# Gate's and up's LoRA by pairs of samples, with B's rows split once and gathered from a table in DRAM

## The reference

```python
# x: 32 samples x 64 positions x 512 features, all float32
x = x + L0(x)      # per sample a 64x64 matrix chosen by itok_B_0_7, and a bias
x = x + L1(x)      # the part that the change touches, adapters chosen by itok_B_0_7:
    base = x @ W ; lora = (x @ A[idx]) @ B[idx]      # rank 16, 8 adapters
    gate, up = lora_linear(x, Wg, Ag, Bg), lora_linear(x, Wu, Au, Bu)   # 512 -> 2048
    y = lora_linear(silu(gate) * up, Wd, Ad, Bd)                        # 2048 -> 512
x = x + L2(x)      # 512x512 matrix and rank-16 adapters chosen by itok_B_0_6
x = x + L3(x)      # per sample a 64x64 matrix chosen by itok_B_1_198
```

## Time and profile before

| | |
|---|---|
| median of 3 runs | 746.84 us (744.89 to 747.26) |
| the profiled execution: time, span | 746.99 us, 745.1 us |
| mean granted clock of TensorE in it | 0.984 |
| units 0 to 7, units 8 to 15 | about 52 to 335 us, about 361 to 635 us |
| before the first unit, and from the last unit on | 52 us, 110 us |

### The profile page before, as it was taken

The page is one execution under the profiler, slowest core; times in us unless marked ns, Lnnn a source line. Parts: engine busy times, 40 slices in busy tenths (PEclk is TensorE's granted clock), DMA queues, the critical chain, the costliest instruction groups (busy, mean ns, idle before and its releaser), DMA issues.

```text
span 745.1 us, 11097 instructions
## 1 busy us (share of the span) xinstructions
PE 713.5 (96%) x3762; PEld 611.7 (82%) x3762; DVE 583.8 (78%) x1008; ACT 289.7 (39%) x526; POOL 289.2 (39%) x537
## 2 busy tenths in 40 slices
PE   8789999999999999989899999999999999879997
PEld 8677788888888888868678888888888888669996
DVE  8868877888887888699898979797878795655553
ACT  3443423343334343334353333342424242335554
POOL 5936423242324232450337162525344331324541
PEclk9899999999999999999999999999999999989999
DMA  8485612121222121413723132222212142203432
GB/s 228 104 139 164 161 57 86 57 85 58 86 84 85 58 86 56 86 29 113 254 75 114 53 106 71 81 80 67 88 62 84 31 130 83 91 11 104 128 113 93
DMA packets 82024, 69.72 MB, mean 94 GB/s; under 512 B 43184, under 2 KB 65712, under 8 KB 81968
## 3 DMA queue, kind: packets, MB, share of 16 engines
q1 hardware_dynamic: 73328, 46.44, 21.5%
q0 software_dynamic: 8320, 22.56, 10.1%
q10 hardware_dynamic: 320, 0.02, 0.0%
HBM read 60.09 MB, written 8.91 MB: 93 GB/s over the span
## 4 chain that ended last, share of the span: by engine, by line
PE 81%; DVE 10%; issue 6%; ACT 2%; DMA 1%; POOL 0%; POOLq 0%; DVEq 0%; ACTq 0%
PE bank L1552 35%; PE bank L1673 21%; PE bank L1560 7%; PE bank L1683 4%; PE bank L1810 3%; PE bank L1816 3%; PE bank L1848 2%; PE bank L1789 1%; DVE XC L1040 1%; PE bank L1505 1%; DVE hid L1164 1%; PE bank L1529 1%; DVE hs L1170 1%; PE bank L1493 1%; DMA BR<-in_L_cond_Bu_dram,boffs 1%
## 5 line engine op out<-in xcount | busy, mean ns | idle before, releaser
L1552 PE MATMUL bank<-XC,WC 128*128 128x512 f32 x1344 | 333.3, 394 | 12.2 <-DVE XC L1040 4.6
L1552 PEld LDWEIGHTS bank<-XC,WC 128*128 128x128 f32 x1344 | 244.4, 189 | 60.8 <-issue 7.0
L1673 PE MATMUL bank<-hs,wds 128*128 128x512 f32 x768 | 190.6, 398 | 6.8 <-DVE wds L1123 4.1
L1673 PEld LDWEIGHTS bank<-hs,wds 128*128 128x128 f32 x768 | 145.2, 192 | 36.9 <-DVE wds L1123 4.5
L464 POOL DMA_INDIRECT BR<-in_L_cond_Bu_dram,boffs x64 | 72.5, 1132 | 253.0 <-DVE BL L1117 238.4
L464 POOL DMA_INDIRECT BR<-in_L_cond_Bg_dram,boffs x64 | 75.8, 1184 | 89.4 <-DVE BL L1117 73.6
L726 ACT ACTIVATE hs<-hid 128x512 fp32r<-128x512 f32 x64 | 40.3, 630 | 164.3 <-DVE hid L1164 109.1
L1181 DVE TENSOR_TENSOR XA<-bank,XA 128x512 f32<-128x512 f32 x128 | 86.4, 686 | 18.6 <-PE bank L1673 16.2
L720 ACT ACTIVATE hid<-hid 128x512 f32<-128x512 f32 x48 | 30.4, 633 | 152.6 <-DVE hid L1147 83.1
L1560 PEld LDWEIGHTS bank<-UT,BL 128*128 128x128 f32 x512 | 76.4, 189 | 9.6 <-issue 0.9
L1560 PE MATMUL bank<-UT,BL 128*128 128x256 f32 x512 | 81.7, 282 | 0.6 <-DVE BL L1117 0.4
(11 more groups left out here) (184 smaller groups left out, 874.7 us busy)
## 6 DMA issues: line engine op xcount, KB each, us to landing
RW<-in_L_cond_Wg_dram SPq DMA_DIRECT2D x16, 512.0 KB, 3.5
RW<-in_L_cond_Wu_dram SPq DMA_DIRECT2D x16, 512.0 KB, 3.5
RD<-in_L_cond_Wd_dram SPq DMA_DIRECT2D x16, 512.0 KB, 3.4
out_dram<-XB SPq DMA_DIRECT2D x16, 256.0 KB, 2.1
XB<-in_x_dram SPq DMA_DIRECT2D x8, 256.0 KB, 6.9
x1park<-XB SPq DMA_DIRECT2D x8, 256.0 KB, 5.0
x2park<-XA SPq DMA_DIRECT2D x8, 256.0 KB, 2.4
XA<-x1park SPq DMA_DIRECT2D x4, 512.0 KB, 6.9
```

What stands on the lines that cost most here:

```text
L1552: last = nc.tensor.matmul(psum[:, :], WC[:, t, left, a, k, :], XC[:, right, b, k, :], start=(first and k == 0 and n == 0), stop=(k == 1 an ...
L1673: last = nc.tensor.matmul(psD[j % 2][:, :], by_feature(wds[:, f, a, :])[:, j % KT, :], hs[:, f, b, j // KT * 512:(j // KT + 1) * 512], sta ...
```

## The change

B's rows are no longer split per window. The rows of Bg and Bu (128 rows of all 8 adapters) are split once per unit index 0 to 7, in one piece of 128x512 (`b_high(unit)`, `b_low(unit)`), and stored high and low to tables in DRAM (`load_b`, `store_b` on SP). `gather_b(b, half)` now fetches for every pair of samples 96 rows, which are high, low and high again of two samples by 16 ranks, straight into `BL`. `BL` has three places; a place holds the 4 pairs of half a window. `UT` holds 96 rows to match (high, high, low of u), so one matmul has all three terms: a call of `lora` is 4 matmuls of 128 columns with weights of 96x128. `select` makes 4 matmuls of 256 columns for what were 2 of 512. The second half of the tokens gathers from the tables that the first half stored.

Some small work moves too: the pair's row numbers are made early on DVE (`pair_rows`), layer 2's B is turned in unit 12 and loaded in unit 8, and `ident2` is made in unit 3.

```diff
-                def gather_b(b):
-                    unit, rows = b // 2, (bg_rows, bu_rows)[b % 2]
-                    if b:
-                        pool.wait_ge(s_bl, 2 * b)
+                def gather_b(b, half):
+                    unit = b // 2
                     h, i = unit // UNITS, unit % UNITS
-                    for q in range(HQ):
-                        at = HQ * h + q
+                    if half == 0 and h == 0 and b % 2 == 0:
+                        pool.wait_ge(s_bst, 32 * (unit + 1))
+                    if b == 0:
+                        if half == 0:
+                            pool.wait_ge(s_poffs, 1)
+                        else:
+                            pool.wait_ge(s_u, 1)
+                    elif half == 0:
+                        if b >= 2:
+                            pool.wait_ge(s_prod, 8 * (b - 2) + 8)
+                        if b == 2 * UNITS:
+                            pool.wait_ge(s_u, 3)
+                    else:
+                        pool.wait_ge(s_prod, 8 * (b - 1) + 7)
+                    place = b_place(b, half)                      # (2 * b + half) % 3
+                    for c in range(HP // 2):
+                        at = HP * h + HP // 2 * half + c
                         nc.gpsimd.indirect_dma_start(
-                            BR[:, q, :], None, rows,
-                            bass.IndirectOffsetOnAxis(boffs[:, at:at + 1].bitcast(u32), 0),
-                            element_offset=i * QT).then_inc(s_br[q // 2], 16)
+                            BL[0:PROWS, place, c, :].bitcast(f32), None, btab[b % 2][i],
+                            bass.IndirectOffsetOnAxis(poffs[0:PROWS, at:at + 1].bitcast(u32), 0)).then_inc(s_bin[place], 16)
...
-                def lora(psum, f, j, tok, first):
-                    for q in range(2):
-                        for a in range(2):
-                            last = nc.tensor.matmul(psum[:, q * QT:(q + 1) * QT], BL[:, a, 2 * tok + q, f * P:(f + 1) * P],
-                                                    UT[:, j, (2 * tok + q) * QT:(2 * tok + q + 1) * QT],
-                                                    start=(first and q == 0 and a == 0), stop=(q == 1 and a == 1),
-                                                    skip_group_check=True)
+                def lora(psum, f, j, tok, b, first):
+                    for c in range(HP // 2):
+                        p = HP // 2 * tok + c
+                        last = nc.tensor.matmul(psum[:, c * P:(c + 1) * P], BL[0:PROWS, b_place(b, tok), c, f * P:(f + 1) * P],
+                                                UT[0:PROWS, j, p * P:(p + 1) * P],
+                                                start=(first and c == 0), stop=(c == HP // 2 - 1), skip_group_check=True)
                     return last
...
-                    b_high(2 * unit + 1, 0)          # ACT, gate_window; b_low(2 * unit + 1, 0) on DVE alike
+                    if unit + 1 < UNITS:
+                        b_high(unit + 1)
```

More of the change, by code:

```diff
@@ L350, in x1_back, with load_b, store_b @@
                         sp.dma_start(XA[:, k, :], x1park[:, k, :]).then_inc(s_x1back, 16)
+                def load_b(unit):
+                    if unit == 1:
+                        sp.wait_ge(s_l0, PAIRS)
+                    elif unit:
+                        sp.wait_ge(s_bl, unit)
+                    for w in range(2):
+                        sp.dma_start(b_raw[min(unit, 1)][:, w, :], b_rows[w][:, unit * QT:(unit + 1) * QT]).then_inc(s_bld, 16)
+                def store_b(unit):
+                    sp.wait_ge(s_bl, unit + 1)
+                    for w in range(2):
+                        sp.dma_start(btab[w][unit].rearrange("(a p) f -> p a f", a=2),
+                                     b_split[min(unit, 1)][:, :, w, :].bitcast(f32)).then_inc(s_bst, 16)
                 load_idx(0, idx_a)
@@ L386, in _ @@
                         load_d(unit + 1)
+                    if unit + 1 < UNITS:
+                        store_b(unit + 1)
+                    if unit + 2 < UNITS:
+                        load_b(unit + 2)
                     if unit + 2 < ALL:
@@ L762, in up_window @@
                     hs_high(unit, 1, 0, 3)
-                    if unit + 1 < ALL and not turn:
-                        b_high(2 * unit + 2, 0)
                     hs_high(unit, 1, 1, 2)
@@ L780, in _ @@
                 xc_high(0, B21)
+                b_high(0)
                 sums_high(G, 0)
@@ L981, in move_matrices @@
                     dve.wait_ge(s_ident, 1)
-                    for half in range(2):
-                        rows = slice(half * POS, (half + 1) * POS)
-                        nc.vector.tensor_copy(ident2[rows, :], ident[rows, rows])
-                    link(nc.vector.memset(moves[:, :, :].bitcast(f32), 0.0))
-                    for j in range(2):
-                        last = nc.vector.tensor_copy(moves[:, 2 * j + 1, :], ident[:, j * HALF:(j + 1) * HALF])
+                    link(nc.vector.memset(moves[:, :, :, :].bitcast(f32), 0.0))
+                    for at in (0, 2):
+                        last = nc.vector.tensor_copy(moves[:, :, at, :], ident[:, :].rearrange("p (c m) -> p c m", c=4))
                     last.then_inc(s_moves, 1)
@@ L1008, in scalings @@
                     dve.wait_ge(s_l0, PAIRS)
+                    for half in range(2):
+                        rows = slice(half * POS, (half + 1) * POS)
+                        nc.vector.tensor_copy(ident2[rows, :], ident[rows, rows])
                     nc.vector.tensor_copy(idxb_f, idx[:, 1, :])
@@ L1220, in gate_window @@
                         hs_low(unit - 1, 0, 1, 4)
-                    b_low(2 * unit, 1)
                     raw_low(U, unit)
@@ L1237, in gate_window @@
                     evicts(unit, slots[1], 0)
-                    b_low(2 * unit + 1, 0)
+                    if unit + 1 < UNITS:
+                        b_low(unit + 1)
                     evicts(unit, slots[1], 1)
@@ L1247, in up_window @@
                         g_combine(unit + 1)
-                    b_low(2 * unit + 1, 1)
                     sum_u2(n)
@@ L1279, in up_window @@
                         xc_low(1, T3)
-                    if unit + 1 < ALL and not turn:
-                        b_low(2 * unit + 2, 0)
                     hs_low(unit, 1, 1, 3)
@@ L1318, in _ @@
                 xr_sum(4)
+                pair_rows()
                 xr_sum(5)
@@ L1324, in _ @@
                 xc_low(0, B21)
+                b_low(0)
                 t2_sum(0)
```

167 lines of the change are left out of this document (93 added, 74 removed).

## The result

The changed kernel takes 740.31 us (median of 4, 739.64 to 742.22) where the kernel before takes 746.27 (4 runs, 744.89 to 747.26): a ratio of 0.9926, 95% interval 0.9900 to 0.9951. The prediction was 740.8 us in a range of 736 to 747. Later the unchanged kernel was run again among the experiments: 739.87 us against 745.83, ratio 0.9921 (0.9906 to 0.9936).

A forecast was written before the change was run, and what follows sets the result against it. PE, busy 96%, was taken to bound the kernel, with DVE late at a few places. Terms -4.1 + 0.2 + 0.1 - 4.5 + 1.8 + 0.4 = -6.1 gave 740.8 us, range 736 to 747.

The forecast's parts named there:

- The columns: PE's `lora` calls: halved columns take each from 0.472 to 0.44 us, -4.1 us over 128 calls.
- the small corrections: On PE: +0.2 us for call gains lost ahead of waits for `sum_u3`, +0.1 for more matmuls in `select`.
- The step's argument: In `lora` calls, successive weight loads stand 100 to 110 ns apart, so matmuls of 60 ns between them don't help.
- DVE's relief: Fewer `b_low` instructions shorten PE's waits for DVE in units 0, 1, 4 and 8: -4.5 us.
- The start: `pair_rows` and `b_low(0)` on busy DVE ahead of the first S2·T2 make PE start later: +1.8 us.
- The gathers: POOL's doubled indirect DMAs fit by 1.3 to 1.9 us in windows without `downs`; one or two late: +0.4 us.
- the first: Rival for `lora` calls: columns are what is paid, -29.7 us instead of -4.1, 715 us; chance 0.05.
- The second: Rival on POOL: gathers are late and the kernel is slower, +12 us, 753 us; chance 0.11.
- the third: Rival: nothing is left; matmuls stay at 118 ns, DVE's relief is -2.2, the start +2.5, 747.4 us; chance 0.14.

The follow-up runs named there:

- e8: The changed kernel, unchanged, run again on another chip: 739.87 us, ratio 0.9921 to the kernel before.
- e3: The kernel before with 128 columns instead of 256 in each LoRA matmul: 742.96 us against 745.6, ratio 0.9956.
- e10: The kernel before with DVE's split of B cut from the second window on and LoRA matmuls at 128 columns instead of 256: 738.50 us, ratio 0.9901.
- e7: The changed kernel without its gathers of B from the fifth window on: 738.69 us, ratio 0.9916.
- e12: The changed kernel with 64 of 128 columns in each LoRA matmul, run again on a fourth chip: 740.72 us, ratio 0.9919.
- e2: The changed kernel with two matmuls of 256 columns a LoRA call instead of four of 128: 760.65 us, with long stalls.
- e9: The kernel before with DVE's split of B cut to 4 of 256 columns from the second window on: 741.07 us, ratio 0.9932.
- e5: The changed kernel with `pair_rows`, the first `b_low` and the first store of B's rows moved later: 739.79 us, ratio 0.9922.
- e1: The changed kernel with 64 of 128 columns in each LoRA matmul: 780.95 us, ratio 1.0455, with long stalls.
- e4: The changed kernel with an idle 512-element DVE instruction wherever the kernel before split B: 783.62 us with long stalls; 748.55 us on a third chip.
- e6: The changed kernel with two more gathers of 32 rows in each of POOL's calls: 763.87 us, ratio 1.0248.
- the first batch: The runs e1, e2, e3 and e4: 780.95, 760.65, 742.96 and 783.62 us; all but e3 had long stalls.

## Why the prediction was right

The medians fell by 5.96 us both times, where -6.1 was forecast. The trace of e8 against that of before, by the same matmuls, shows the terms. Its span is 8.1 us shorter. Of this 1.5 is a stretch of half clock in layer 3 that the one execution had and the other had not; +0.6 had come by 43 us, and -7.1 comes from there to the end of the units. The first profile of the change has the same -7.1 there, but stands at +2.4 by 43 us.

- **The columns**: predicted -4.1 and the small corrections +0.3; by the units with `downs` it is 16 x -0.16 = -2.6. A call fell by 33 ns against the 32 expected, when it is read to its third follower, and e3's units fell by 30 ns a call. In the changed kernel, though, 0.08 us in each unit (0.04 in each hundred matmuls, 1.3 in all) come back against e10's pace, spread over the 512-column matmuls of the products. It isn't the gathers' traffic (e7); whether it is the 96 rows or the order of instructions isn't settled. This is the term most in error. The step's argument, that loads and not columns set the price, is shown by e3, by e12 and the 909 ns at 64 and 128 columns, and by e2, where two loads fewer took 200 ns from a call. Every matmul here has a load of its own, so a price of the pair that isn't the load's would look the same; that the recorded loads stand 112 ns apart speaks for the load.
- **DVE's relief**: predicted -4.5; what the units lost beyond their 0.16 us sums to -4.6: -1.8 in units 0 and 1 (predicted -1.8), -0.1 in unit 3, -1.1 in unit 4 (-0.7), -1.6 in units 7 to 9 (-2.0). Unit 4 fell by another 0.5 us, but that is the turn of layer 2's B itself, which costs the same 0.5 in unit 12 now. Unit 4 had two late places, not one: its ads (0.24 us of waiting at 194 us) and `sum_u2`. In unit 8 the second `b_low` was partly taken back, since PE reaches the sum sooner and still waits 0.66; the wait at 384.78, which the prediction puts in unit 8, stands in unit 9. e9, which takes only DVE's part away, has -3.1 of this. The rest went with ACT's copies, with PE's own waits for `BL`, or with the order of instructions; no run tells them apart.
- **The start**: predicted +1.8, for DVE's added instructions alone. They cost a little less: from the matmul at 17.87 us before (17.77 in e8) to S2·T2, the nine profiles that have the change's order on DVE take 14.1 to 14.2 us, and the four of the old order and e5, which has the instructions elsewhere, 12.7. PE in order of time in e8, where the kernel before has no wait at the first two:
```profile
19.03 1.13 PE L1561 MATMUL bank<-w0second,udp 128*128 128x128 f32 x8 [0.42 <-DVE XA L1095]
...
20.77 1.13 PE L1561 MATMUL bank<-w0second,udp 128*128 128x128 f32 x8 [0.18 <-DVE XA L1095]
...
31.98 2.90 PE L1611 MATMUL bank<-XC,WC 128*128 128x512 f32 x6 [5.26 <-DVE XC L1100]
```
`pair_rows` stands ahead of a sum of layer 0 that PE already waits for at 19 and 21 us, which is why the wait ahead of S2·T2 grew by 0.6 and not by 1.8.

Two more things move the matmul at 43 us. First, x comes later in every profile with the change: by 1.1 us in the first against the kernel before, and on the same chip by 0.6 in e1, e2 and e4 against e3, and by 0.1 and 0.6 in e8 and e5 against e9 and e10. `load_b(0)` stands among the loads of x, and the prediction gave it nothing; no run moves it, so whether it is the cause is open. Second, the half clock behind S2·T2 ends sooner in e8 than in the kernel before (35.1 and 35.5 us, though S2·T2 started later), so that the 24 matmuls of L1585 take 3.23 us instead of 4.03. In all, against the same kernels, the matmul at 43 us comes 2.4 us later in the first profile, 1.5 to 1.6 in e1, e2 and e4, and 1.0 to 1.1 in e8. So the step "so PE starts 1.8 us later, and with it all that follows" held as far as S2·T2, at 1.4 to 1.5 us. Moving these instructions away gains nothing even so: in e5 POOL's copies and the half clock took what DVE gave back.

- **The gathers**: predicted +0.4; no wait of PE is for one. They land in 2.7 us instead of 3.5, and take POOL 1.00 us each. The margin in the windows without `downs` was real, and e6 used it up.
- **The rivals**: the first is excluded by e3 and e12. The second did not come; e6, which forces it, has its waits where the prediction looked for them, and half clock behind the larger ones, which the price of +12 us didn't hold. Of the third, the start came in part (2.4 us in one profile), the other terms did not.

That the sum came out within 0.2 us of the change is in part that its errors cancel: the columns brought 1.2 us less than forecast, the gathers cost 0.4 less, and the start, by what is left of the medians' -5.96, some 0.6 less. The medians' difference itself is known to about 1 to 2 us.

## What to carry to other kernels

In this kernel a short matmul with weights of its own costs its load: 110 to 115 ns at 128 columns of weights, whether 64 or 128 columns stream, and 118 to 120 ns when 256 stream. So fewer matmuls are worth more than fewer columns: two in place of four gave 200 ns a call, halved columns 33. Work taken from a busy engine counts at the few places where PE waits for it, to the tenth of a microsecond there and not at all elsewhere; list these places and what is late next at each. Where one engine is full and another's chain ends at nearly the same time, time taken from the first is worth only what lies between the two: e5 took 1.5 us from DVE's queue and won nothing at 43 us. Give DMAs that are put among the loads of the start a price of their own, and look at more than one profile before a difference of 1 us at the start is believed.

## What the hardware showed

Two executions of the same kernel differ in three places alone. From 60 to 635 us the first profile of the changed kernel and e8's stay 1.68 to 1.76 us apart, but for a moment at the turn between the halves. Of that, 1.2 comes by 19 us, while x arrives, and 0.6 behind S2·T2, where the half clock lasts until 37.6 us in one and 35.1 in the other. A further 1.5 us comes at one place in layer 3. The windows of that stretch in the two (columns as in the earlier trace rows):
```profile
662.30:669.10 6.80, 6.80 (x41) 6.66 (x42) 2.81 (x5) 2.17 (x5) 2.43 (x4) 0.75 0.20 67
```
```profile
659.00:665.80 6.80, 5.73 (x42) 5.45 (x43) 4.08 (x7) 2.65 (x6) 3.51 (x7) 1.00 0.24 67
```
The granted clock is 0.75 in one (3.4 us at 1.2 GHz) and 1.00 in the other, behind the same short waits of 1.3 and 0.4 us. A difference of 1.5 us between two kernels' single profiles can be this alone.

The stalls of the first batch stay open. The same two kernels took 780.95 and 783.62 us there and 740.72 and 748.55 us elsewhere, so these kernels don't always have them; the kernel before and e3 ran undisturbed in the same batch, and the changed kernel itself was not run on that chip. What holds ACT for 2 to 8 us, and whether the denser gathers make a kernel open to it, no run here tells.
